# First batch of a state space block: ScalarE scales the transposed states, TensorE adds them in PSUM, in place of VectorE's sums

## The reference

```python
def ssm(hidden, z, ...):                      # 4 batches, 512 steps, 512 channels, 16 states
    u = silu(conv4(in_proj_w @ hidden) + conv_b)
    dt_lo, Bm, Cm = split(x_proj_w @ u)
    delta = softplus(dt_proj_w @ dt_lo + dt_proj_b)
    for t in range(512):
        state = state * exp(delta_t * A) + (delta_t * u_t) * B_t
        y_t = sum over n of state[:, n] * C_t[n]
    return ((y + D * u) * silu(z)).T

x = x + tanh(g_xattn) * ssm(ctx, layernorm(x), ...)
h = layernorm(x)
x = x + tanh(g_ffn) * (shared_expert(h) + sum over the top 3 of 7 experts of w_e * expert_e(h))
# expert(h) = (silu(h @ W1) * (h @ Wg)) @ W2
```

## Time and profile before

| | |
|---|---|
| median of three runs | 1540.28 us |
| profiled execution, its own time | 1539.44 us |
| its span (first to last instruction) | 1537.3 us |
| TensorE busy in the span | 1369.0 us (89%) |
| VectorE busy | 1092.0 us (71%) |
| ScalarE busy | 473.2 us (31%) |
| mean granted TensorE clock | 0.933 |

### The profile page before, as it was taken

How to read it: one execution, slowest core, us unless ns; L and a number is a source line. 1 busy time by engine, 2 the same in 40 slices (tenths; PEclk the granted TensorE clock), 3 DMA queues, 4 the chain that set the end, 5 groups by cost and what they waited for, 6 DMA issues and landing times.

```text
span 1537.3 us, 18479 instructions
## 1 busy us (share of the span) xinstructions
PE 1369.0 (89%) x6183; PEld 1071.7 (70%) x6183; DVE 1092.0 (71%) x1323; ACT 473.2 (31%) x795; POOL 453.9 (30%) x240
## 2 busy tenths in 40 slices
PE   8555459999999996999999986999999999999999
PEld 4333337777777774787777864787777878888887
DVE  5899985799998965579999955579999962322222
ACT  3633214644343312432223212433223211111111
POOL 3200004477777730022233310023233311111111
PEclk9687569999999997999999997999999999999999
DMA  6111272676665554365555564365555564665552
GB/s 204 38 55 54 93 263 112 221 257 236 235 230 207 202 211 173 111 213 177 163 169 175 168 224 139 117 210 178 166 167 177 166 220 136 215 210 193 195 169 82
DMA packets 90806, 266.43 MB, mean 173 GB/s; under 512 B 11472, under 2 KB 11600, under 8 KB 90336
## 3 DMA queue, kind: packets, MB, share of 16 engines
q1 hardware_dynamic: 85472, 258.39, 49.5%
q10 hardware_dynamic: 5248, 6.96, 1.3%
HBM read 207.39 MB, written 57.93 MB: 173 GB/s over the span
## 4 chain that ended last, share of the span: by engine, by line
PE 67%; DVE 22%; issue 6%; ACT 2%; DMA 2%; SPq 1%; DVEq 0%; ACTq 0%; POOL 0%
PE ps_hg L452 19%; PE ps_h L452 18%; PE ps_y L452 12%; DVE st L1059 10%; PE ps_y L591 8%; DVE y_rows L1065 5%; PE ps_mid L517 4%; DVE st L1050 3%; PE ps_mid L499 1%; PE ps_mid L495 1%; PE ps_mid L492 1%; DMA st<-xin_scratch 1%; DVE h_tmp L1174 1%; DVE h_tmp L1179 1%; DMA w_raw<-in_Ws_dram 1%
## 5 line engine op out<-in xcount | busy, mean ns | idle before, releaser
L1312 POOL TENSOR_TENSOR h_lo<-h_tmp,h_hi 128x512 fp32r<-128x512 f32 x128 | 280.8, 2193 | 799.3 <-ACT h_hi L827 799.3
L452 PE MATMUL ps_h<-x_hi,w_split 128*128 128x512 f32 x1024 | 352.5, 406 | 7.0 <-DVE x_lo L1106 4.3
L452 PE MATMUL ps_hg<-x_hi,wg_split 128*128 128x512 f32 x1024 | 348.8, 402 | 0.0
L1059 DVE TENSOR_TENSOR_SCAN st<-dA,st 128x1024 f32<-128x1024 f32 x128 | 298.2, 2330 | 0.0
L517 PE MATMUL ps_mid<-ident,st 128*128 128x128 f32 x1024 | 173.8, 300 | 94.0 <-DVE st L1059 49.6
L452 PE MATMUL ps_y<-w_split,h_hi 128*128 128x512 f32 x1024 | 256.4, 398 | 0.8 <-ACT h_hi L827 0.8
L517 PEld LDWEIGHTS ps_mid<-ident,st 128*128 128x128 f32 x1024 | 132.5, 153 | 153.8 <-DVE st L1059 92.4
L452 PEld LDWEIGHTS ps_h<-x_hi,w_split 128*128 128x128 f32 x1024 | 196.3, 192 | 49.4 <-issue 4.9
L452 PEld LDWEIGHTS ps_hg<-x_hi,wg_split 128*128 128x128 f32 x1024 | 194.7, 190 | 40.8 <-issue 0.3
L1174 DVE SCALAR_TENSOR_TENSOR h_tmp<-h_tmp,ps_h 128x512 f32<-128x512 f32 x128 | 87.8, 686 | 183.2 <-ACT h_tmp L821 182.5
L452 PEld LDWEIGHTS ps_y<-w_split,h_hi 128*128 128x128 f32 x1024 | 189.0, 189 | 39.6 <-ACT h_hi L827 2.0
(11 more groups left out here) (122 smaller groups left out, 1018.1 us busy)
## 6 DMA issues: line engine op xcount, KB each, us to landing
w_split<-split_scratch SPq DMA_DIRECT2D x192, 512.0 KB, 4.8
wg_split<-split_scratch SPq DMA_DIRECT2D x96, 512.0 KB, 4.2
split_scratch<-w_split SPq DMA_DIRECT2D x64, 512.0 KB, 4.2
b_all<-xd_scratch SPq DMA_DIRECT2D x64, 256.0 KB, 3.8
split_scratch<-wg_split SPq DMA_DIRECT2D x32, 512.0 KB, 3.1
w_raw<-in_W_dram SPq DMA_DIRECT2D x14, 1024.0 KB, 7.8
wg_raw<-in_Wg_dram SPq DMA_DIRECT2D x7, 1024.0 KB, 10.0
dA<-in_x_dram SPq DMA_DIRECT2D x4, 1024.0 KB, 8.5
```

What stands on the lines that cost most here:

```text
L452: mm = pe.matmul(out_, lhs[a], rhs[c], start=first and q == 0, stop=last and q == len(sides) - 1)
L1059: dve.tensor_tensor_scan(flat[1], flat[0], flat[1], 0.0, ALU.mult, ALU.add).then_inc(scan_done, 1)
L1312: pool.tensor_tensor(h_lo[:, j, :], h_tmp[j % 2][:], h_hi[:, j, :].bitcast(F32), ALU.subtract).then_inc(hl_ready, 1)
```

## The change

In batch 0 alone:

- The sums leave VectorE. ScalarE's `first_scale` multiplies a transposed tile by C on its way from `ps_mid` to `y_rows`, and TensorE's `first_add` adds `y_rows` onto a PSUM bank by a matmul with the identity. The four sums over n stand in the four banks `first_y` (the convolution's banks, free by then).
- u * D goes straight into these banks (`first_init`), so the four `init` uses of `ps_mid` and ScalarE's four copies go. The sixteen small matmuls now stand together ahead of `dt0`.
- VectorE runs bmul, bmul, scan, scan for each n. Ahead of the first bmul of n it waits until the last transposes of n - 2 are done.
- ScalarE's order for each n becomes: two decays of n + 2, four scalings of n, two decays of n + 2, then `stage`.
- `first_make_y` reads the sums from PSUM.
- `keep_warm` ahead of the columns writes another bank, behind a wait for `in_staged`.

Core of the diff (helpers that only pass `m` to the place functions are left out):

```diff
+        first_y = conv_ps
...
+        FIRST_FRONT = [name for name in FRONT if not name.startswith("init")]
...
+            def first_init(i):
+
+                for et in range(T):
+                    mm = pe.matmul(first_y[i][:, et * P:(et + 1) * P], u[:, et, i * P:(i + 1) * P], diag_D[:, et, :],
+                                   start=et == 0, stop=False)
+                mm.then_inc(init_done, 1)
+
+            def first_add(n, i):
+
+                pe.wait_ge(*taken(0, sum_place(0, n, i)))
+                pe.matmul(first_y[i][:], ident[:], y_rows[:, i, :], start=False, stop=n == DS - 1).then_inc(first_sum, 1)
...
-            front(0, *FRONT)
+            front(0, "xproj")
+            for i in range(T):
+                first_init(i)
+            front(0, *FIRST_FRONT[1:])
             for n in range(DS):
-                for i in range(T):
+                state_to_rows(0, n, 0)
+                for i in range(1, T):
                     state_to_rows(0, n, i)
+                    first_add(n, i - 1)
+                first_add(n, T - 1)
                 if n < 2 * T:
                     in_proj(2 + n // T, n % T)
-            keep_warm(WARM_NORM, ps_h1[0])
+            pe.wait_ge(in_staged, T * (NB - 1))
+            keep_warm(WARM_NORM, ps_y[1])
...
+            def first_scale(n, i):
+
+                bank, before = mid(0, sum_place(0, n, i))
+                if n:
+                    act.wait_ge(first_sum, T * (n - 1) + i + 1)
+                act.wait_ge(mid_done[bank], before + 1)
+                act.activation(y_rows[:, i, :], ps_mid[bank][:], ACT.Copy, scale=c_cols[:, i, n:n + 1]).then_inc(mid_read[bank], 1)
...
-            for n in range(2, DS):
-                decays(0, T * n, T * (n + 1))
-                if 0 <= n - 3 < 2 * T:
-                    stage(2 + (n - 3) // T, (n - 3) % T)
+            for n in range(DS):
+                decays(0, T * (n + 2), T * (n + 2) + 2)
+                for i in range(T):
+                    first_scale(n, i)
+                decays(0, T * (n + 2) + 2, T * (n + 3))
+                if 0 <= n - 1 < 2 * T:
+                    stage(2 + (n - 1) // T, (n - 1) % T)
...
+            def first_make_y():
+                for i in range(T):
+                    dve.wait_ge(first_sum, T * (DS - 1) + i + 1)
+                    dve.scalar_tensor_tensor(out=y_rows[:, i, :], in0=first_y[i][:], scalar=half_tgx[:, 0:1],
+                                             in1=z2[:, i, :], op0=ALU.mult, op1=ALU.mult).then_inc(y_ready, 1)
...
-            for n in range(1, DS + 1):
-                for r in range(T):
-                    slot(0, n, r)
-            slot(0, DS + 1, 0)
-            make_y(0, range(T))
+            for n in range(1, DS):
+                if n >= 2:
+                    bank, before = mid(0, sum_place(0, n - 2, T - 1))
+                    dve.wait_ge(mid_done[bank], before + 1)
+                for h in range(2):
+                    bmul(0, n, h)
+                for h in range(2):
+                    scan(0, n, h)
+            first_make_y()
```

More of the change, by code:

```diff
@@ L246, in mid_router, with front_names, front_place, sum_place @@
             return place, MID_FIRST // 2 + MID_TURN // 2 * b
[L248 to L255, removed]
+        def front_names(m):
+            return FRONT if some(m) else FIRST_FRONT
+        def front_place(m, name):
+            return front_names(m).index(name)
+        def sum_place(m, n, i):
+            return len(front_names(m)) + T * n + i
+        def column_place(m, i):
+            return len(front_names(m)) + T * DS + i
         @block.sync
@@ L521, in x2_to_columns @@
                 for i in range(T):
-                    bank, before = mid(m, column_place(i))
+                    bank, before = mid(m, column_place(m, i))
                     pe.wait_ge(x2_ready, T * m + i + 1)
@@ L709, in front_z @@
                 for i in tiles:
-                    bank, before = mid(m, front_place(f"z{i}"))
+                    bank, before = mid(m, front_place(m, f"z{i}"))
                     act.wait_ge(mid_done[bank], before + 1)
@@ L717, in front_init @@
                     act.wait_ge(x1_ready, T * m)
-                bank, before = mid(m, front_place(f"init{i}"))
+                bank, before = mid(m, front_place(m, f"init{i}"))
                 act.wait_ge(mid_done[bank], before + 1)
@@ L722, in front_xd @@
             def front_xd(m):
-                bank, before = mid(m, front_place("xproj"))
+                bank, before = mid(m, front_place(m, "xproj"))
                 act.wait_ge(mid_done[bank], before + 1)
@@ L729, in front_ccols @@
             def front_ccols(m):
-                bank, before = mid(m, front_place("ccols"))
+                bank, before = mid(m, front_place(m, "ccols"))
                 act.wait_ge(mid_done[bank], before + 1)
@@ L739, in front_dt @@
                     act.wait_ge(u_ready, T * (m + 1))
-                bank, before = mid(m, front_place(f"dt{et}"))
+                bank, before = mid(m, front_place(m, f"dt{et}"))
                 act.wait_ge(mid_done[bank], before + 1)
@@ L932, in _ @@
                 front_dt(0, et)
-                front_init(0, et)
             front_ln(0, range(T))
@@ L1037, in front_du @@
                 dve.wait_ge(delta_ready, T * (m + 1))
-                dve.wait_ge(*taken(m, front_place("init3")))
-                dve.wait_ge(*taken(m, front_place("xproj")))
+                if some(m):
+                    dve.wait_ge(*taken(m, front_place(m, "init3")))
+                else:
+                    dve.wait_ge(init_done, T)
+                dve.wait_ge(*taken(m, front_place(m, "xproj")))
                 dve.scalar_tensor_tensor(out=u[:], in0=delta[:], scalar=0.5, in1=u[:],
@@ L1061, in sum_rows @@
             def sum_rows(m, n, i):
-                bank, before = mid(m, sum_place(n, i))
+                bank, before = mid(m, sum_place(m, n, i))
                 dve.wait_ge(mid_done[bank], before + 1)
```

26 lines of the change are left out of this document (12 added, 14 removed).

## The result

The changed kernel took 1516.24 us (median of four runs, 1514.88 to 1517.36) against 1540.82 for the kernel before: the ratio is 0.9843, with a 95% interval of 0.9825 to 0.986. That is 24.6 us less; forecast were 28.5 less (1511), with a range of 1501 to 1524. The profiled execution took 1515.26 us with a span of 1513.2, so its gain is 24.2 us and the forecast for it (1510.9) was 4.3 us too low.

The account below looks back on a forecast made before the run. VectorE was taken to bound batch 0's state space stretch. 28.0 us earlier at batch 1's convolution plus 0.5 at the front make 28.5 off the profiled 1539.44: 1510.9, called 1511, range 1501 to 1524.

Parts of the forecast that it names:

- The step that bounds: Batch 0's state space loop: VectorE sets the round; without the sums its 9.27 us fall to 6.67.
- The two further waits: Loop's start: VectorE, ready near 72.5 and 81.1 us, starts bmuls of n = 2 and 3 at 74.4 and 81.85.
- ScalarE's order makes a chain: Rounds with in_proj: scalings, adds, transposes, decays and stage in one chain take 7.65 us, for seven rounds.
- TensorE's own chain: Rounds with in_proj: TensorE's 7.04 us of work plus its wait for the first scaling, 7.4 us.
- The slow-clock rival: Loop: TensorE's clock stays low, half throughout from n = 9, so the kernel is slower, 1557 us; chance 0.06.
- from n = 9 TensorE's chain is 5.7 and ScalarE's 6.7 or less: Rounds without in_proj: both chains are short enough that VectorE's 6.67 us is the bound again.
- The two bounds that the prediction held apart: Batch 1's convolution, from the end of n = 13's bmul: VectorE's rows ready at +33.1 us, the input allows +35.4.
- The front: Ahead of the loop: ScalarE loses four copies, sixteen small matmuls stand ahead of dt0; gain 0.2 to 1.9, taken 0.5 us.
- The fully covered case: Rival, loop: ScalarE and TensorE keep up, rounds 6.67 us from n = 1, convolution 37.5 us early, 1501 us; chance 0.10.
- The hand-offs: Rival, loop: eight passes between ScalarE and TensorE cost 0.14 us more each, rounds 8.8 us, 1519 us; chance 0.17.
- the case of nothing gained: Rival, behind the loop: stores behind the last load of B don't move with it, queue takes the gain, 1539; chance 0.02.
- The signs: Loop and behind: listed trace marks, such as 7.65 us rounds; wrong if clock falls, adds exceed 1 us or VectorE never waits.

Follow-up runs that it names:

- e10: Changed kernel with the edits of e1, e9, e6 and e5, plus in_proj in rounds 0, 2, 4, 6, 8, 10, 12, 13: 1502.43 us.
- e1: Changed kernel with ScalarE's loop order turned: scalings 0 and 1, one decay, scaling 2, one decay, scaling 3, two decays, stage: 1511.55 us.
- e9: e1 with in_proj moved inside the round, between the second tile's transposes and the first add: 1506.94 us.
- e3: Changed kernel with eight matmuls without a use in TensorE's idle time of n = 9: 1514.56 us.
- e6: Changed kernel with ScalarE's split of the first down weights, and GpSimd's four subtractions with it, moved ahead of the loop: 1513.2 us.
- e2: Changed kernel with in_proj in rounds 0, 2, 4, 6, 8, 10, 12, 13 instead of 0 to 7, stage one round behind each: 1531.19 us.
- e5: e1 with the twelve stores of split weights spread behind the loads of B of n = 5 to 12: 1511.09 us.
- e4: Changed kernel without TensorE's adds of n = 0 to 14, all of ScalarE's scalings kept: 1504.59 us.

## Why the prediction was right, point by point

**The step that bounds, and its size.** VectorE's 6.67 us is measured as 6.63 where nothing else binds (e10), the sums are gone from the path, and VectorE waited at the first bmul for the transposes of n - 2 in all seven rounds forecast at 7.65. The wait is 1.07 (0.9 to 1 expected), the round 7.81 (7.65). The two further waits that it had at the loop's start, ahead of the bmuls of n = 2 and n = 3, did not come: VectorE was itself too late for them.

**Who makes the round.** "ScalarE's order makes a chain", 7.65, and "TensorE's own chain", 7.4: this comparison failed. TensorE's adds step by 0.95 us on average and not 0.86, its wait for the first scaling is 0.40 in the profile and 0.57 from start to start (1.44 less 0.87), where 0.38 was counted, and its chain is 7.81. Turning ScalarE's order left the round as it was (e1), filling TensorE's wait shortened it (e9). That 7.65 is so near to 7.81 is in part luck: it is the sum of a chain that did not bind. By the chain that did, at its forecast 7.4, the time would have been some 1.8 us lower (7 x 0.25) and further off.

**Where the missing 4.3 us are.** From the loop's start, forecast and measured: bmul of n = 3 at 16.7 and 17.5 (0.8 late); bmul of n = 10 at 70.2 and 72.1 (1.1 more, seven rounds by 0.16); end of the bmul of n = 13 at 92.5 and 97.4 (3.0 more); the convolution at 127.9 and 132.0 (0.8 given back). The start itself lay 0.5 us earlier than forecast, and 0.8 came behind the convolution, which stays open. In e3, with the same code up to there, the bmul of n = 10 came at 71.4, so some 0.7 of the 1.9 us up to there differ from one execution to the next.

- *0.8 us: VectorE and GpSimd.* The prediction kept the surcharge of the kernel before for these rounds. Without the sums more of VectorE's time falls beside GpSimd's work, 4.2 us in two rounds and not 1.6. They alternate with GpSimd's, as the rows at e6 show; the sums with their input in PSUM did not take part. Part of it hid the start's low clock: with it gone (e6) TensorE was late by 0.4 us.
- *3.0 us: the seam at n = 9.* By e3 1.7 of them are the clock and 1.0 the late scaling at full clock; the rest is 0.04 us in each round behind it. The slow-clock rival was priced for the whole loop only. It came true in one round, at the seam between two regimes: "from n = 9 TensorE's chain is 5.7 and ScalarE's 6.7 or less" overlooked that the first such round inherits ScalarE's `stage`. e3 and e2 show it from both sides, and with the turned order of e1 the wait is gone altogether.
- *Behind the loop.* The two bounds that the prediction held apart (33.1 and 35.4 us) came out together at 34.4 and 34.6. VectorE was later, because TensorE stayed behind to the end: ScalarE's chain of 6.7 us is as long as VectorE's round, so TensorE's delay never drained. The first y came 3.72 us after the last scan, and 2.71 with the turned order.
- *The input and the queue.* The input's landing kept its distance to the backlog (33.8 us from the end of the bmul of n = 13, against 34.6 before) and not to its own issue (7.7 us, against 5.6). By that count it was issued 2.9 us earlier than before (at 26.1, against 29.0) and was there 0.8 earlier. In e1 it was issued at 24.9 and was there at 33.9, 9.0 us behind its issue. The Trainium skill's rule (DMA: Bandwidth & Descriptors, Queues, rings and completion order), that descriptors of one issuing engine's row are taken in ring order, agrees with this: with the stores moved ahead (e5), it was there 5.2 us after its issue.

**The front.** 0.5 us was forecast. In seven traces with the changed front the loop starts at 64.2 to 66.7, 65.6 on average, against 65.2 before: no gain can be claimed. What moves this start from run to run stays open.

**The rivals.** The fully covered case needs the five edits of e10: 37.4 us earlier at the convolution and 1502.4, where the rival had 37.5 and 1501. The hand-offs were short: about 0.1 us from the transposes to a scaling (103.70 to 103.80). The stores did move with the last load of B, so the case of nothing gained did not come.

**The signs.** Right were the waits of about 1 us, the rounds of 6.7 behind them, x's rows ahead of the residual (there at 184.7, used from 187.5) and the first tap waiting for the input. Wrong were "no idle time on ScalarE" (1.14 and 0.61 us in each round, which its own sum of 6 us in 7.65 had implied), adds at 0.86, VectorE idle for some 2 us ahead of the convolution (0.20), and a clock of 1.00 to the last add. The prediction named a fall of the clock in the loop as a sign of being wrong, and it fell, for some 4 us. The time held because that happened in one round only.

## What to carry to other kernels

When work is moved off a bound engine, draw the chain that the move creates between the others and look at its seams: the first round of a new regime still waits for what the last one queued. A wait on TensorE can cost more than its length where the clock falls behind it, as at n = 9, where that was 1.7 us more. e2 moved work to even out TensorE's sums and lost 15 us; an estimate from e3 is that the clock is some 10 of them (six such rounds at 1.7). In an in-order engine, put work that is ready (decays, `in_proj`) into the gaps of the hand-off chain rather than around it.

## What the hardware showed

- *The clock.* An idle time of 2.1 us on TensorE behind continuous work at full clock was followed by a stretch at half (granted 0.66, then 0.50); waits of 0.40 us in every round (1.00 in all stretches of e1 from 85 to 185 us) and of 1.0 us (1.00 in the change from 147 us on) were not. The length of the wait does not decide it alone: in e4, where TensorE has no adds, waits of 2.2 to 3.2 us in each round from 84 to 111 us left the clock at 1.00, and in the kernel before a wait of 2.21 us ended at 99.43 with the clock full and one of the same length at 108.70 with it at half.
- *VectorE beside GpSimd.* Beside GpSimd's subtractions a bmul took 2.2 to 2.3 us in place of 1.20 and a scan 3.3 in place of 2.28; the first subtraction took 1.27 us and the last 3.25. From the second on, each ended about one length of its own behind the other engine's. In the kernel before, VectorE's sums stayed at 0.72 to 0.75 us in the same stretch. The Trainium skill (SBUF — State Buffer, Who interferes with whom) has a rule for this: VectorE contends with a GpSimd instruction that reads SBUF where both of its inputs come from SBUF. The rows agree: bmul and scan have two such inputs, the sum has one in PSUM.
- *An add behind a wait costs more.* A float32 add of 128x512 steps by 0.86 us in a stream. It steps by 0.96 where it had to wait for ScalarE (the first and the fourth): there its weight load starts with it and not ahead of it (at 102.14 and 105.84, against 103.43 for the add at 103.54). The third add's 1.00 holds the fourth's wait for its scaling.
